# Perceiver attention rewritten: pairs of heads in 64-row tiles, keys two blocks ahead, GpSimd adds

## The reference, cut to what matters

```python
z = concat(norm(context), norm(latents))          # 7428 x 128
for h in range(16):
    q, key, value = latents @ Wq[h], z @ Wk[h], z @ Wv[h]     # 64 columns each
    s = q @ key.T
    p = exp((s - max(s, axis=-1)) / 8)
    x += (p @ value / sum(p, axis=-1)) @ Wo[h]
```

## Time and profile before

| | us |
|---|---|
| median of 3 runs | 4276.89 (4273.33 to 4277.46) |
| the profiled execution, its own time | 4278.51 |
| its span, first to last instruction | 4276.8 |
| PE busy | 3753.6 (88%) |
| DVE busy | 3274.7 (77%) |
| ACT busy | 2087.3 (49%) |
| POOL busy | 1123.1 (26%) |
| mean granted TensorE clock | 0.916 of full speed |

### The profile page before, as it was taken

The page is one execution under the profiler, slowest core; times in us unless marked ns, Lnnn a source line. Parts: engine busy times, 40 slices in busy tenths (PEclk is TensorE's granted clock), DMA queues, the critical chain, the costliest instruction groups (busy, mean ns, idle before and its releaser), DMA issues. The chain is left out here.

```text
span 4276.8 us, 73742 instructions
## 1 busy us (share of the span) xinstructions
PE 3753.6 (88%) x17107; PEld 2135.2 (50%) x17107; DVE 3274.7 (77%) x4967; ACT 2087.3 (49%) x4475; POOL 1123.1 (26%) x1776
## 2 busy tenths in 40 slices
PE   3978888484358999999999999999999999999997
PEld 2545455232345555555555555555555555555545
DVE  6878787553177898889789788888978988888752
ACT  3323333242145475566457556655744755664442
POOL 1222222211201232323223233232322323332330
PEclk8989988565669999999999999999999999999997
DMA  1000000000300000000000000000000000000000
GB/s 51 0 0 0 0 0 0 10 1 35 93 3 2 1 2 2 0 2 0 2 2 0 2 0 2 2 0 2 0 2 2 0 2 0 2 0 1 0 1 26
DMA packets 21262, 26.78 MB, mean 6 GB/s; under 512 B 3016, under 2 KB 13392, under 8 KB 21072
## 3 DMA queue, kind: packets, MB, share of 16 engines
q1 hardware_dynamic: 19856, 22.88, 1.7%
q0 software_dynamic: 1344, 3.15, 0.3%
HBM read 22.35 MB, written 3.67 MB: 6 GB/s over the span
## 5 line engine op out<-in xcount | busy, mean ns | idle before, releaser
L1916 DVE TENSOR_REDUCE peaks<-banks 128x512 f32 (+1 forms) x1856 | 1196.9, 687 | 208.7 <-PE banks L1764 203.1
L1877 ACT ACTIVATE probs<-banks 128x512 f32<-128x512 f32 x1856 | 1004.4, 593 | 647.0 <-PE banks L1724 642.1
L1926 DVE TENSOR_TENSOR probs_total<-probs_total,probs 128x1024 f32<-128x1024 f32 x896 | 1172.3, 1308 | 49.3 <-ACT probs L1877 49.3
L1743 PE MATMUL banks<-probs,value_step 128*64 128x512 f32 x3712 | 1010.5, 623 | 3.7 <-ACT value_step L1706 3.2
L1764 PEld LDWEIGHTS banks<-keys,query_high_high 128*128 128x128 f32 x3712 | 515.5, 193 | 765.2 <-issue 524.2
L1723 PE MATMUL banks<-query_high_high,key_high_low 128*128 128x512 f32 (+1 forms) x1888 | 774.7, 410 | 25.2 <-ACT query_low_shift L2006 24.5
L1764 PE MATMUL banks<-keys,query_high_high 128*128 (+1 forms) x3712 | 718.9, 315 | 45.0 <-DVE peaks L1916 31.6
L1724 PE MATMUL banks<-query_low_shift,key_high_one 128*128 128x512 f32 (+1 forms) x1888 | 743.5, 394 | 0.0
L1686 POOL CAST key_high_low<-keys 128x256 fp32r x480 | 245.7, 512 | 1545.6 <-PE banks L1724 1278.1
L1686 POOL CAST key_high_one<-keys 64x256 fp32r x480 | 547.8, 1141 | 0.0
L1723 PEld LDWEIGHTS banks<-query_high_high,key_high_low 128*128 128x128 f32 (+1 forms) x1888 | 353.6, 187 | 129.6 <-ACT probs L1877 53.6
(11 more groups left out here) (316 smaller groups left out, 3407.8 us busy)
## 6 DMA issues: line engine op xcount, KB each, us to landing
expert_w<-in_fc SPq DMA_DIRECT2D x32, 256.0 KB, 4.0
context_rows<-in_ctx SPq DMA_DIRECT2D x10, 320.0 KB, 6.1
dense_w<-in_We SPq DMA_DIRECT2D x2, 1024.0 KB
experts_in<-expert_zeros SPq DMA_DIRECT2D x1, 1024.0 KB, 3.9
expert_b<-in_fc_b SPq DMA_DIRECT2D x2, 512.0 KB, 4.7
expert_rows<-experts_in SPq DMA_DIRECT2D x16, 64.0 KB, 2.0
experts_out<-expert_result POOLq DMA_DIRECT2D x4, 256.0 KB, 4.7
wq<-in_wq SPq DMA_DIRECT2D x16, 64.0 KB, 1.7
```

Of the source, the lines that this page charges most:

```text
L1743: last = pe.matmul(out[a * HD1:(a + 1) * HD1, c, :], value[:, r, a, :], probs[:, 2 * c + a, :], start=start, stop=last_step and a != c)
L1877: inc("expd", act.activation(probs[:, 2 * c + a, :], scores[:, a, :], ACT.Exp, scale=1.0 / 8.0))
L1916: inc("peak", v.reduce_max(peaks[:, 2 * f:2 * f + 2, ds(j, 1)].rearrange("p t o -> p (t o)"), fills[:, f % 2, :].rearrange("p (n w) -> p n ...
L1926: inc("counted", v.tensor_tensor(total[:, units, :], total[:, units, :], probs[:, units, :], ALU.add))
```

## The change

`perceiver_attention` is written anew, with its order in `perceiver_order`. Nothing else is changed but that `rows` and `squares` are given back before the stage, to make room.

- **Pairs of heads.** Head 0 of a pair lies in rows 0 to 63 and head 1 in rows 64 to 127 of queries and keys. All matmuls of scores and fills have 64 rows. A score is four of them: ones with the negated maximum, high with high, low keys with high queries, high keys with low queries (L1842). The two heads alternate and write different banks. GpSimd stages no keys any more.
- **A fill inside a score entry.** A score entry is one key tile of 128 with 512 queries and both heads: eight matmuls. A fill of the next pair (L1823) is one matmul of 512 keys for each head, and its two parts stand inside and behind the entry. In an odd step the fourth fill stands alone behind `produce`.
- **A step** is two key tiles of both heads. The products (L1868) of the two tiles of the step before follow each other behind the scores: 8 matmuls, the two heads in the two halves of 64 columns.
- **Keys and values** come in blocks of 512 (`produce`, L1807 and L1813), two blocks ahead, kept in a ring of 17 blocks.
- **Sums.** VectorE adds 5 and GpSimd 3 of every 8 tiles of 1024 exponentials (`by_pool`), each into its own total. GpSimd also multiplies the output by the reciprocals (L2051).
- **At a pair's end** the sums over partitions are spread over 64 columns for each head, so the reciprocal (L2021) has 1024 columns instead of 8.
- The first pair's fills, 120 of two parts, run alone. The whole is straight-line code, with no loop.

```diff
+def perceiver_order():
+
+    order = [("queries", 0), ("queries", 1), ("produce", 0, 0, None, None)]
...
+    for g in range(PAIRS):
+        more, most = g + 1 < PAIRS, g + 2 < PAIRS
+        for s in range(STEPS1 + 1):
+            tiles = (2 * s, 2 * s + 1) if s < STEPS1 else (TILES,)
+            fills = []
+            if more and s < 2 * (BLOCKS - 2):
+                fills = [("fill", g + 1, s // 2, 4 * (s % 2) + n) for n in range(4)]
+            elif more and s < 2 * (BLOCKS - 1):
+                fills = [("fill", g + 1, BLOCKS - 2 + s % 2, t) for t in range(TT)]
+            parts = [(i, c) for i in tiles for c in range(2)]
+            inside = len(fills) // 4
+            late = fills[-1:] if inside == 1 else []
+            for n, (i, c) in enumerate(parts):
+                own = fills[n * inside:(n + 1) * inside] if inside else []
+                if late and n == 3:
+                    own = []
+                order.append(("scores", g, i, c, own[0] if own else None))
+                order += own[1:]
+            if s % 2 == 1 and s < 2 * (BLOCKS - 2):
+                order.append(("produce", g + 1 if more else None, s // 2 + 1, g, s // 2 + 1))
+            elif s == 2 * (BLOCKS - 2) and more:
+                order.append(("produce", g + 1, BLOCKS - 1, None, None))
+            elif s == 2 * (BLOCKS - 2) + 1:
+                order.append(("produce", None, None, g, BLOCKS - 1))
+            elif s == STEPS1 - 1 and more:
+                order += [("peak", g + 1), ("shift", g + 1)]
+            elif s == STEPS1 and more:
+                if most:
+                    order.append(("queries", g + 2))
+                order.append(("produce", g + 2 if most else None, 0, g + 1, 0))
+            order += late
+            if s == 0:
+                if g:
+                    order += [("denominators", g - 1), ("add", g - 1, TILES), ("evacuate", g - 1)]
+            else:
+                order += [("add", g, 2 * s - 2), ("add", g, 2 * s - 1)]
+            if s == 2 and g:
+                order.append(("output", g - 1))
+            order += [("sum", g, i, c) for i, c in parts]
+    g = PAIRS - 1
+    order += [("denominators", g), ("add", g, TILES), ("evacuate", g), ("output", g)]
+    return order
...
+    by_pool = lambda i, c: c == 1 and i < TILES and (i % 2 == 1 or i // 2 % 2 == 1)
...
+                def wait_free(e):
+                    n = place[e] - 2
+                    if n < 0:
+                        return
...
+                def fill(f, head):
+                    g, b, t = f[1:]
+                    if head == 0:
+                        wait(pe, "qhigh", number["queries", g])
+                        wait(pe, "high", keys_of[g, b])
+                    wait(pe, "peaked", 2 * fill_number[f] + head - 1)
+                    pe.matmul(fill_banks[:, head, 0:width(b)], q_high[g % 2][heads[head], t * P:(t + 1) * P],
+                              k_high[heads[head], (g * BLOCKS + b) % RING1, 0:width(b)], start=True,
+                              stop=True).then_inc(S["filled"].sem, 1)
...
+                    def product(head, m):
+                        left = (one_rows[heads[head], 0:n], k_high[heads[head], r, columns],
+                                k_low[heads[head], r, columns], k_high[heads[head], r, columns])[m]
+                        right = (q_shift, q_high, q_high, q_low)[m][g % 2][heads[head], cols]
+                        return pe.matmul(slot(e)[0:n, head, :], left, right, start=m == 0, stop=m == 3)
+
+                    product(0, 0)
+                    product(1, 0)
+                    if f is not None:
+                        fill(f, 0)
+                    for m in range(1, 4):
+                        if f is not None:
+                            last = product(1, m)
+                            last = product(0, m)
+                        else:
+                            last = product(0, m)
+                            last = product(1, m)
+                    last.then_inc(S["made"].sem, 1)
+                    if f is not None:
+                        fill(f, 1)
...
+                    for c in range(2):
+                        for head in range(2):
+                            last = pe.matmul(out[heads[head], c, :], values[0:n, (g * BLOCKS + i // 4) % 2, i % 4, heads[head]],
+                                             probs_of(i)[0:n, c, head, :], start=i == 0, stop=i == TILES)
+                    last.then_inc(S["added"].sem, 1)
...
+                    for c in range(2):
+                        for head in range(2):
+                            last = pe.matmul(slot(e)[heads[head], c, :], k.ones[:, 0:HD1], total[:, c, head, :],
+                                             start=True, stop=c == 0)
...
+                    elif e[0] == "denominators":
+                        wait_made(v, e)
+                        if e[1]:
+                            wait(v, "scaled", e[1])
+                        v.reciprocal(inverse[:].rearrange("p (b c) -> p b c", b=2),
+                                     slot(e)).then_inc(S["inverted"].sem, 1)
...
-            for rows_, tile in ((slice(0, P), key_a), (slice(0, HD1), key_b)):
-                inc("staged", pool.tensor_copy(tile[rows_, r, :], keys[hp][rows_, ds(j * STEP, STEP)]))
-            pe.matmul(scores[rows_, bank, :], key_a[:, r, keys_], q_a[hp][:, cols], start=True, stop=False)
-            return pe.matmul(scores[rows_, bank, :], key_b[:, r, keys_], q_b[hp][:, cols], start=False, stop=True)
-                inc("score", score_unit(pe, hp, r, slice(a * P, (a + 1) * P), a, c))
-                inc("score", score_unit(pe, hp, NS % 2, slice(0, LAST), c, c), 2)
```

More of the change, by code:

```diff
@@ L2079, in next_pair @@
[L2079 to L2089 removed]
+                v.memset(one_rows[:].bitcast(F32), 0.0).then_inc(S["cleared"].sem, 1)
+                v.memset(peak[:], 0.0).then_inc(S["cleared"].sem, 1)
@@ L2091, in perceiver_attention @@
+                wait(v, "cleared", 2)
+                for row in (0, HD1):
+                    v.memset(one_rows[row:row + 1].bitcast(F32), 1.0).then_inc(S["cleared"].sem, 1)
+                wait(v, "cleared", 4)
         with nc.Block() as block:
```

801 lines of the change are left out of this document (326 added, 475 removed).

## The result

The changed kernel takes 4368.23 us (median of 4 runs, 4359.93 to 4375.74), the kernel before 4277.18 (4 runs, 4273.33 to 4281.17). The ratio is 1.021, with a 95% interval of 1.020 to 1.022. It is **slower by 2.1%**, clear of the noise (whether by more than 2% the interval leaves open), where 4006 us and "faster" were forecast, and it lies outside the range. The profiled execution took 4365.01 us, span 4363.3.

The account below looks back on a forecast made before the run. TensorE's own work was taken to bound the kernel. Block 18.6 + 0.9 + 0.8 = 20.3 us; stage 190 + 7 x 321 + 243 + 16 = 2696 for 2967, giving 4006 us, range 3830 to 4200.

Parts of the forecast that it names:

- the second loss of VectorE: In each block, a GpSimd sum getting in between VectorE's sums costs VectorE 2.0 us, of which 0.8 is charged.
- B: Rival: VectorE and GpSimd together bound the kernel, a whole GpSimd sum entering VectorE's order; block 22.2 us, kernel 4190, chance 0.18.
- D: Rival: waits for VectorE lower TensorE's clock to a mean 0.9 in the pairs; 250 us more, kernel 4260, chance 0.05.
- TensorE in a block: TensorE's work for four key tiles of a head pair: scores, fills, products, keys and values, 18.6 us against 22.6 before.
- Side by side and a hidden load: 64-row score and fill matmuls overlap in two row halves with weight loads hidden: 80 matmuls take 9.2 us a block.
- rival C: Weight loads between 64-row score and fill matmuls are not hidden: 500 us more before offsets, kernel 4410 to 4510, chance 0.07.
- pacing: In score entries holding a fill, VectorE's two reads take 1.29 us against TensorE's 1.15; 0.9 us lost a block.
- The pair: Two heads together: 14 blocks at 284 us, plus 4, 12.9, 11.9 and 8 for its end, 321 us against 361.
- The reciprocal: At a pair's end, VectorE's reciprocal over 1024 columns takes 6.5 us and stalls TensorE 8 us in all.
- The last pair: Final two heads, with no fills or keys to make: blocks of 15.9 us, 243 us with its end.
- two score slots: Score buffering against ScalarE's exponentials: two slots suffice while an entry is above 1.0 us, so ScalarE is covered.
- The start: Before the first score, 120 fills at 1.4 us make 168; with queries, first keys and turning 190 us against 119.

Follow-up runs that it names:

- the clock experiment: Changed kernel with 8 pairs of redundant matmuls filling TensorE's wait before the second part of each long step, nothing else moved: 4280.19 us.
- all the edits: Changed kernel plus sooner GpSimd sums, reciprocal in pieces, multiply moved later, output added behind the sums, and four fill banks in the start: 4025.33 us.

## Why the prediction was wrong

**The step that failed** is the second loss of VectorE: "I charge 0.8 of it, not the whole". The place was right, sums behind the reads just when GpSimd's last sum gets ready, and the duration nearly (2.41 us for 2.0, with bounds 1.22 to 3.2). What it does was undersized twice. The hold is 1.71 us in every full block and reaches TensorE in full, since the scale above is 1 to 1; nothing of it is made good. And the wait that it makes costs TensorE its clock, 1.34 us more in 65 of 78 long steps. Together 2.8 us a block against 0.8.

**The rivals B and D stood apart, and came together.** B gave 22.2 us a block for the hold alone; the steps of 13.31 and 9.15 make 22.46. D gave a mean clock of 0.9 in the pairs; it was 0.94. I priced each by itself at 4190 and 4260 and gave them 0.18 and 0.05. But D's cause is B's wait: with B's hold came D, in 65 of 78 blocks. (With the quarters' shorter hold TensorE waits 1.51 us in the same place, and the clock stayed full.) The case "B and then D" had no number; with the 88 us that the clock experiment gives it would have been 4190 and some 90 more, 4280, and what is left to the measured time lies in the start and at the ends of pairs, below. The range was drawn to reach B alone and so ended at 4200.

**TensorE in a block.** Side by side and a hidden load: right. Pairs of 64-row matmuls come 0.23 us apart in a run of eight, so rival C is out. By the Trainium skill, page "TensorE: Matmul & The Clock Gate", Part 3, "The mechanism", a weight load overlaps matmuls in flight only where the row group differs. The 0.23 us agree with that: with the two heads in turn, no load makes a gap. One visit of products takes 3.65 us (3.7 forecast). The block without any hold is 20.75 (sooner sums) or 20.55 (no sums on GpSimd), where PE with pacing had been put at 19.5. The profile of the latter shows where: three of the four parts of a step hold a fill that waits for its read, and come 1.3 to 1.6 us apart instead of 1.15, though PE is then counted busy.

**GpSimd.** 2.41 us for 1024 columns. The estimate from the GPSIMD Engine Reference of the Trainium skill, section 3.1, was 2.3, nearer than my 2.0. The page "SBUF — State Buffer" of the Trainium skill, section "SBUF: two separate sides", has the shared pair held for a whole instruction: the quarters agree, and so does the sum of 3.12 us that outlasts GpSimd's by 1.08. Its section "Who interferes with whom" says that a VectorE instruction with at most one SBUF input, outside the 2-port modes, does not contend with GpSimd; the traces agree for the reads of PSUM, 0.68 to 0.69 us each with or without a GpSimd sum beside them.

**The pair.** Forecast 321 us, measured 366.0. With the sooner sums it is 334.2 (from 1753.5 to 3758.5, six pairs), so the collision is 31.8 of the 45. With all the edits 324.6 (1697.6 to 3644.9): the boundary's queues are 9.6. The last block of a pair, charged 4 us for its 16 fills, takes 28.1 us where a full block takes 20.75 (both with the sooner sums), 7.3 more. The reciprocal lasts 6.56 us (6.5 forecast) and costs 8.4 with what it delays (8 forecast). The wait of VectorE for the output product was not in the sum at all.

**The last pair**: 258.8 for 243. A block takes 17.26 us for 15.9. In blocks without keys and fills TensorE waits some 0.2 us for ScalarE's exponentials (1.03 us each) ahead of up to every second entry. I had called two score slots enough "as long as an entry is above 1.0 us"; without fills an entry is 0.93. These waits come to some 0.6 of the 1.4 us; the rest was not separated.

**The start**, up to the first score: 227 for 190. I took 1.4 us for a fill, between 1.29 and 1.8. It was 1.64, and the clock 0.51 where the same kind of stretch had 0.80, so the keys took 2.07 and each block of 8 fills 15.2 us. With four banks it is 173.

**The sum.** Start +37, first pair +39 (360 us from the first score to its sums over partitions), six pairs +270, last pair +16, the end +1, together 363; the rest of the kernel is some 5 us shorter than before, and the profiled execution took 4365 where 4007 was forecast, 358 more. By causes: 223 us are the one collision, 37 the start, and the 98 left are pacing, boundaries between pairs, the first and the last pair. With the collision, the queues at the boundary and the start mended, the same change gives 4025 us, near the 4006 forecast. That nearness is in part luck: the start is 17 us shorter there than forecast, and the pairs are longer.

Open: why 13 long steps kept the clock with the same wait of some 2.07 us in them, and why the clock stays low in the start with PE 91% busy.

## What to carry to other kernels

Before giving work to GpSimd, look at when it starts, not only how long it takes: beside VectorE's reads of PSUM it was nearly free (4145 us with the sums sooner, 4129 with none at all), beside VectorE's sums it stopped VectorE, and one changed condition was worth 5%. Where a case makes TensorE wait, price the clock behind the wait as part of that case, not as a rival to it. In orders written out by hand, ask of each waiting entry what stands behind it: three of the gains here (multiply, addition of the output, reciprocal) were queues behind a wait or a long instruction.

## What the runs showed that was not expected

- Work that computes nothing made the kernel 88 us faster: 2.0 us of redundant matmuls in a gap of about that length keep the clock, and what follows runs at full rate.
- The same did not work in the start: PE went from 78% to 91% busy by redundant fills, and the granted clock only from 0.51 to 0.55.
- VectorE's copy of 1024 columns from SBUF takes 0.63 to 0.69 us where GpSimd is quiet, about half its sum's 1.22, but 1.64 in the mean of the changed kernel, since the second copy at a pair's end meets GpSimd's multiply and takes 2.83.
- GpSimd's sum in four quarters takes 2.80 us instead of 2.4 beside reads of PSUM, and this small loss bought 133 us: a shorter hold, and with it TensorE kept its clock.
- Spreading VectorE's sums made the full blocks shorter and the last block of each pair longer, so the kernel's time alone (23 us) understates what the order does to a block.
